# Moving the second half of a context load behind the first group of key-stacking transfers

## The reference, cut to what matters

```
k = _split_heads(key @ Wk.T + bk)        # key = value = ctx_1024, (32, 1601, 256)
v = _split_heads(value @ Wv.T + bv)
score = jnp.einsum('bhqd,bhkd->bhqk', q, k) * SCALE
attn = jax.nn.softmax(score, axis=-1)
out = jnp.einsum('bhqk,bhkd->bhqd', attn, v)
```

## Time and profile before

| what | value |
| --- | --- |
| median of 3 runs | 1980.44 us (1973.1 to 1981.19) |
| profiled execution, its own time | 1994.08 us |
| its span | 1992.2 us |
| PE busy, whole span | 1891.7 us (95%) |
| PEld busy (weight loads) | 1781.0 us (89%) |
| DVE busy | 1468.1 us (74%) |
| ACT busy | 1109.3 us (56%) |
| POOL busy | 896.8 us (45%) |
| SP's DMA queue, share of 16 DMA engines | 55.0% |
| granted TensorE clock, mean | 0.979 |

### The profile page before, as it was taken

The page is one execution under the profiler, slowest core; times in us unless marked ns, Lnnn a source line. Parts: engine busy times, 40 slices in busy tenths (PEclk is TensorE's granted clock), DMA queues, the critical chain, the costliest instruction groups (busy, mean ns, idle before and its releaser), DMA issues. The chain is left out here.

```text
span 1992.2 us, 46867 instructions
## 1 busy us (share of the span) xinstructions
PE 1891.7 (95%) x18796; PEld 1781.0 (89%) x18796; DVE 1468.1 (74%) x2741; ACT 1109.3 (56%) x1850; POOL 896.8 (45%) x1032
## 2 busy tenths in 40 slices
PE   7899999999999999999999999999979789999998
PEld 5899999999989989999999989899957689999998
DVE  6777787878777787877777787878745577666667
ACT  2555556556555655555655555565664435666652
POOL 3224254533424353543424362533235135888960
PEclk9899999999999999999999999999989789999999
DMA  8656566666656666555666665666542225666633
GB/s 270 163 146 160 146 179 172 157 154 155 160 142 156 180 166 155 149 152 150 160 155 167 161 163 151 156 155 154 123 139 73 72 106 187 223 221 211 234 116 133
DMA packets 151864, 317.41 MB, mean 159 GB/s; under 512 B 58032, under 2 KB 82736, under 8 KB 148192
## 3 DMA queue, kind: packets, MB, share of 16 engines
q1 hardware_dynamic: 146272, 300.41, 55.0%
q0 software_dynamic: 4224, 11.54, 1.9%
q10 hardware_dynamic: 1152, 2.47, 0.5%
HBM read 135.90 MB, written 20.19 MB: 78 GB/s over the span
## 5 line engine op out<-in xcount | busy, mean ns | idle before, releaser
L502 ACT COPY a_pT<-a_pst 128x512 f32<-128x512 f32 x768 | 422.2, 584 | 421.6 <-PE a_pst L941 421.5
L508 ACT ACTIVATE a_probs<-a_probs,a_nmax 128x1601 f32<-128x1601 f32 x256 | 418.8, 1636 | 184.0 <-DVE a_probs L633 184.0
L633 DVE TENSOR_SCALAR_CACHE_REDUCE a_probs<-a_pss 128x1608 f32<-128x1608 f32 x256 | 467.3, 1825 | 12.2 <-PE a_pss L930 12.1
L941 PE MATMUL a_pst<-a_id,a_probs 128*128 128x128 f32 (+1 forms) x3328 | 458.9, 277 | 11.9 <-ACT a_pT L502 9.2
L941 PEld LDWEIGHTS a_pst<-a_id,a_probs 128*128 128x128 f32 (+1 forms) x3328 | 384.9, 142 | 56.0 <-issue 29.7
L364 POOL TENSOR_TENSOR a_tick<-a_tick 128x1 f32<-128x1 f32 x62 | 13.6, 219 | 751.1 <-DMA a_raw<-in_ctxT 657.2
L651 DVE TENSOR_SCALAR a_khi<-a_psk,a_bk 128x402 fp32r<-128x402 f32 x250 | 158.5, 634 | 169.4 <-PE a_psk L895 135.6
L893 PE MATMUL a_pso<-a_whi,a_chi 128*128 128x256 f32 (+1 forms) x806 | 244.9, 304 | 21.7 <-DVE a_v L658 20.2
L369 POOL TENSOR_TENSOR a_clo<-a_raw,a_chi 128x402 fp32r<-128x402 f32 x240 | 248.8, 1068 | 4.8
L930 PE MATMUL a_pss<-a_kst,a_bd 96*128 96x402 f32 x1024 | 241.6, 358 | 5.7 <-DVE a_v L658 5.7
L895 PE MATMUL a_pso<-a_whi,a_clo 128*128 128x256 f32 (+1 forms) x806 | 228.5, 284 | 0.0
(11 more groups left out here) (246 smaller groups left out, 3721.7 us busy)
## 6 DMA issues: line engine op xcount, KB each, us to landing
a_kst<-a_khi SPq DMA_DIRECT2D x1008, 100.5 KB, 2.3
a_kst<-a_klo SPq DMA_DIRECT2D x504, 100.5 KB, 2.4
a_raw<-in_ctxT SPq DMA_DIRECT2D x60, 804.0 KB, 5.7
f_gur<-in_wgu SPq DMA_DIRECT2D x24, 1408.0 KB, 6.3
f_dr<-in_wd SPq DMA_DIRECT2D x24, 768.0 KB, 7.3
a_bd<-q_scr SPq DMA_DIRECT2D x192, 32.0 KB, 2.0
e_big<-ys_scr SPq DMA_DIRECT2D x8, 512.0 KB, 8.0
a_pT<-in_ctxT SPq DMA_DIRECT2D x2, 1608.0 KB, 8.7
```

Source lines behind the costliest of these rows:

```text
L502: nc.scalar.copy(pT[:, p % HALF, 4 * i:4 * i + 4, :], ps_t[:, i % 2, :].rearrange("p (t q) -> p t q", q=P)).then_inc(t_copied_act, 1)
L508: nc.scalar.activation(pr, pr, ACT.Exp, bias=nmax[:, b, p:p + 1], scale=-1.0, accum_out=esum[:, b, p:p + 1]).then_inc(probs_ready, 1)
L633: nc.vector.tensor_scalar(probs[:, p % 2, :].rearrange("p (b k) -> p b k", b=QK), ps_s[:, :, 0:KQ], -SCALE, None, ALU.mult, ALU.min, accum ...
L941: mm = nc.tensor.transpose(ps_t[0:r, i % 2, (t % 4) * P:(t % 4 + 1) * P], probs[:, p % 2, t * P:t * P + r], a_id_sb[:])
```

## The change

The load of half 1 of the context of batch n+2 is taken from its place behind the load of half 0 and is issued between groups (0,0) and (0,1) of the key stacking.

```
                     if not last:
 
                         sp.wait_ge(kv_filled, STEPS * (n + 1))
-                        for k in range(NC):
-                            load_ctx(n + 2, k)
+                        load_ctx(n + 2, 0)
                     if b == 0 and it > 1:
...
                     if ahead:
                         stack_keys(n + 1, 0, 0)
+                    if not last:
+                        load_ctx(n + 2, 1)
+                    if ahead:
                         stack_keys(n + 1, 0, 1)
```

## The result

The changed kernel takes 1955.91 us as the median of 4 runs (1955.11 to 1960.86), the kernel before 1980.53 us (1973.1 to 1981.19). The ratio is 0.9879 with a 95% interval of 0.9852 to 0.9906: 24.6 us or 1.2% faster. Forecast were 1970 us and a range from 1960 to 1984. The sign was right, the gain more than twice the forecast 10.5 us, and the time lies outside the range.

A forecast was written before the change was run, and what follows sets the result against it. The prediction took PE as the bound, with 32.1 us idle in the steady part. 12 us for Pattern A less 1.5 for Shared access gave 10.5 us off 1980.4, so 1970 us; range 1960 to 1984.

The forecast's parts named there:

- What bounds the kernel: Steady attention, 60 to 1400 us: PE is the bound, and any gain lies in its 32.1 us of idle time.
- Pattern A: Slot 4, mostly even batches: DVE waits for late group (0,0), then PE for DVE; removing it wins 12 us (8.7 to 15.3).
- backlog: Context load ahead of group (0,0): 0.8 of 1.6 MB go, so its last DMA lands at most 1.8 us sooner, generally.
- issue slot: On SP, group (0,0) starts one load issue earlier: 0.43 us at the median, at most 1.46.
- Rival 1: Group (0,0): the backlog stays, only the issue slot counts, 3.6 us gained: 1977 us; chance 0.18.
- POOL and group (0,1): POOL splits half 1 about 4 us later and group (0,1) stands behind that load; both cost nothing.
- Shared access: POOL's second cast in even batches may hold up DVE's L693: 4 hits in 14, charged at 1.5 us.
- Rival 3: Even batches: the second cast meets L693 in every one, 7 us slower, 1988 us; chance 0.08.
- Rival 2: Without a profile running the waits may be under the 1.5 us PE doesn't notice: no gain, 1980 us; chance 0.10.
- Pattern B: Slot 3, odd batches: PE waits after cumulate, lengthened when POOL's cast catches scan or L739; stays near 20 us.
- rival 4: Odd batches: number of hits changes at 2.3 us each; fewer: 1961 us, chance 0.11; more: 1984 us, chance 0.06.

The follow-up runs named there:

- run 3: Against the changed kernel: half 1 is issued behind group (0,0) in even batches only, in odd ones ahead of it as before; 1970.87 us, ratio 0.9948.
- run 6: Against the changed kernel: group (0,0) of odd batches held back until the scores of slot 3 are done; 1971.85 us, one run.
- run 1: Against the kernel before: in odd batches POOL starts the split of half 0 only when DVE's cumulate is done; 1971.81 us, ratio 0.9958.
- run 8: Against the changed kernel: cumulate moved from the end of slot 2 of odd batches to slot 0, ahead of the normalisation; 1942.06 us, ratio 0.9808.

## Why the prediction was right and wrong

- **What bounds the kernel:** right in part. PE is the bound, and 19.7 of its 32.1 us of idle time are gone. But "whatever the change can win lies in the 32.1 us" is wrong: PE's busy time for the same matmuls fell by 16 us. The prediction read the mean clock of 0.99 as the upper level throughout; it held seven falls.
- **Pattern A, backlog and issue slot:** right in kind. The group lands 2.7 us earlier (forecast 2.2): the issue brought 1.2 us in place of 0.43, some 0.5 of them because half 0 itself is issued earlier in the batch (11.2 in place of 11.7 us in the mean), and the transfer 1.5 in place of 1.8. Worth 10.3 us in the even batches alone, by run 3 (4 to 17 by the interval); forecast 12 for all. Rival 1, by which only the issue slot counts, is refuted: more than half of the 2.7 us came from the shorter landing.
- **POOL and group (0,1):** both cost nothing, as said; DVE waits 0.7 us for stacking in all. L677 (now L679), which the prediction held to be freed, isn't: the median of its 64 is 448 ns, before 293.
- **Shared access, L693:** the 4 hits charged at 1.5 us didn't happen, 0.41 us each. Rival 3 is refuted for this kernel.
- **Rival 2, nothing outside a profile:** refuted by the medians.
- **Pattern B: the step that failed.** The prediction read the collision of cast and scan rightly, priced it at 2.3 us a hit, and said of the half that stays ahead of the group that it "now travels alone". From that it took pattern B as unchanged ("Pattern B stays near 20 us") and put its move in a rival with a chance of 0.11 for fewer hits. In the runs half 0 of odd batches lands later (5.1 us or more, before 4.4 to 5.3), since group (0,0) follows it directly; run 6 parts them and the collisions return. The number of hits went from 8 of 14 to none. At 2.3 us each that is 18 us of the 25.8 of the odd batches in the profile, and five falls of the clock are in this price. By run 1, which takes away the collisions alone, it is 8.3 us of the median, with an interval from 3 to 14. That the hits became fewer and not more, as rival 4 allowed too, followed from no step of the prediction.

The prediction took over the 13.6 us between the profiled execution and the median unchanged. Most of them are the clock: the profiled execution had a mean of 0.979, the 31 others had 0.984 in the median, and the difference is worth an estimated 10 us over the span. So the profiled execution was rich in falls, and the gain read from it, 39 us, is more than the 24.6 us of the medians. The executions of the kernel before spread over 27 us, those of the changed kernel over 8, which fits a number of hits that differs from one execution to the next. Hits were counted in profiled executions only, so this is argued and not shown.

The forecast was the sum of a well-measured term and a term left at zero because the trace said "nothing" about its sign. Rival 4 had 0.17 in all for a mechanism worth 9 to 18 us; with no hit at all it gives 18 us more, 1952 us, and the range should have reached down to that.

The Trainium skill, "SBUF — State Buffer", section "Who interferes with whom", says that a DVE instruction with two SBUF inputs contends with a GpSimd instruction that reads SBUF. Scan, L739 and L693 of the earlier trace rows behave so; the scan took 0.68 us alone and 2.06 us beside a cast.

## What to carry to other kernels

When a transfer moves, ask of each of its neighbours what stands directly behind it now: half 0 was neither moved nor issued later, and its later landing brought half of the gain. Where two engines hold each other up, write down by how much they miss each other; if it is under 1 us, as here, a change elsewhere in the loop can decide it. Moving the instruction to a slot with slack (run 8: 14 us) is safer than to trust in the spacing. Look at the clock behind the long waits of PE, and not at its mean alone: a wait of 1.9 us cost some 1.7 us more where a fall followed. And what a wait is named at isn't its price: 8.4 us of waits were worth 14 in run 8, while run 1 took away 11.7 us (20.2 less 8.5) and gained 8.

## What the runs showed that was not expected

- A load of 804 KB took 4.4 to 5.3 us to land with another of its kind directly behind it, and 5.1 to 9.5 us with twelve transfers of 100.5 KB directly behind it; with these held back until 2.2 to 4.3 us behind it, mostly 4.3 to 4.8 us again. So transfers issued later can delay one issued earlier. Why the large one behind it doesn't wasn't tested.
- DVE's scan of 256 elements took 0.68 us alone and up to 2.06 us with a cast on POOL.
- The granted clock fell to 0.50 for 3.4 us at a time behind single waits of PE of 1.4 to 2.7 us, seven times in the steady part of the kernel before; three waits of 1.8 to 2.0 us had none behind them.
